# Three blocks of exponents, longer rings for h and u, and ScalarE's long stages in parts, in a selective-scan layer on one core

## What is computed

```
x = layernorm(x + scan(x));  x = layernorm(x + ffn(x))       # x: 2 x 1024 x 512

scan: xn = rmsnorm(x) * norm_w;  xn *= sigmoid((xn @ sel.T + b) * gate)
      delta, B, C = split(xn @ x_proj.T)                     # 128 each
      dt = softplus(delta @ dt_proj.T + dt_b);  A = -exp(A_log)   # A: 512 x 128
      for each of 1024 tokens:                               # h: 2 x 512 x 128
          h = exp(dt * A) * h + (dt * x) * B
          y = sum over the 128 states of h * C
      out = (y + x * D) @ out_proj.T
ffn:  (silu(x @ w_gate.T) * (x @ w_up.T)) @ w_down.T         # hidden 2048
```

## Time and profile before

| | us |
|---|---|
| three runs | 2697.46, 2687.02, 2690.41; median 2690.41 |
| the profiled execution | 2687.74 |
| its span | 2685.9 |
| VectorE busy | 2584.4 (96%) |
| TensorE busy | 2316.6 (86%) |
| ScalarE busy | 1708.6 (64%) |
| GpSimd busy | 1028.3 (38%) |

### The profile page before, as it was taken

How to read it: one execution, slowest core, us unless ns; L and a number is a source line. 1 busy time by engine, 2 the same in 40 slices (tenths; PEclk the granted TensorE clock), 3 DMA queues, 4 the chain that set the end, 5 groups by cost and what they waited for, 6 DMA issues and landing times.

```text
span 2685.9 us, 48350 instructions
## 1 busy us (share of the span) xinstructions
PE 2316.6 (86%) x17036; PEld 1290.5 (48%) x17036; DVE 2584.4 (96%) x4160; ACT 1708.6 (64%) x2229; POOL 1028.3 (38%) x1031
## 2 busy tenths in 40 slices
PE   7866678998789987899779997799977998899998
PEld 4322224554345543555345553455534554465567
DVE  6999999999999999999999999999999999999892
ACT  5687766667566665667656666566666667654643
POOL 2343333443434434344333443344333443344320
PEclk8999999999999989999889998899989999999899
DMA  4566665777667876678757786577866777788694
GB/s 171 197 213 227 228 236 211 281 277 270 237 223 277 284 266 223 238 275 292 254 195 247 279 290 243 201 267 277 278 241 209 279 279 271 239 289 308 228 357 151
DMA packets 192060, 672.16 MB, mean 250 GB/s; under 512 B 20944, under 2 KB 26064, under 8 KB 191824
## 3 DMA queue, kind: packets, MB, share of 16 engines
q1 hardware_dynamic: 152432, 544.02, 57.5%
q10 hardware_dynamic: 39392, 125.06, 13.3%
HBM read 660.61 MB, written 8.39 MB: 249 GB/s over the span
## 4 chain that ended last, share of the span: by engine, by line
PE 39%; DVE 28%; ACT 15%; issue 12%; DMA 6%; POOL 0%; ACTq 0%; DVEq 0%; POOLq 0%
DVE h L709 14%; PE banks L1200 11%; DVE banks L686 10%; PE banks L1036 10%; PE banks L1176 7%; PE banks L1276 7%; ACT a L981 6%; DVE h L706 4%; DMA u_bc<-u_scratch 4%; ACT L720 2%; DMA U<-in_xT 1%; PE banks L1128 1%; PE banks L1124 1%; ACT u_bc L1000 1%; ACT v L862 1%
## 5 line engine op out<-in xcount | busy, mean ns | idle before, releaser
L981 ACT ACTIVATE a<-banks 128x2048 f32<-128x2048 f32 x512 | 960.7, 1876 | 604.3 <-PE banks L1200 563.1
L686 DVE TENSOR_TENSOR banks<-a,h 128x512 f32<-128x512 f32 x2048 | 1324.1, 688 | 4.1 <-ACT a L981 4.1
L709 DVE SCALAR_TENSOR_TENSOR h<-u_bc,BCt,banks 128x512 f32<-128x512 f32 x1482 | 1038.2, 732 | 5.4 <-PE banks L1276 5.4
L581 POOL TENSOR_TENSOR dexp<-spread,dt 128x512 f32<-128x512 f32 x512 | 539.1, 1053 | 821.2 <-DVE banks L686 779.2
L1200 PE MATMUL banks<-dexp,A 32*128 32x256 f32 x8192 | 623.6, 421 | 150.6 <-ACT a L981 149.0
L1276 PE MATMUL banks<-h,cz 128*32 128x512 f32 x4096 | 667.9, 623 | 94.4 <-DVE h L706 64.7
L1200 PEld LDWEIGHTS banks<-dexp,A 32*128 32x128 f32 x8192 | 390.3, 195 | 484.4 <-ACT a L981 347.7
L1036 PE MATMUL banks<-vT,w_ring 128*128 128x256 f32 x1792 | 449.9, 394 | 7.6 <-ACT up L948 6.9
L1036 PEld LDWEIGHTS banks<-vT,w_ring 128*128 128x128 f32 x1792 | 323.8, 190 | 175.4 <-issue 118.2
L706 DVE TENSOR_TENSOR h<-u_bc,banks 128x512 f32<-128x512 f32 x566 | 367.5, 673 | 19.9 <-PE banks L1276 19.9
L593 POOL TENSOR_SCALAR u_bc<-u_bc,BCt 128x512 f32<-128x512 f32 x266 | 184.1, 692 | 404.6 <-DVE banks L686 394.3
(11 more groups left out here) (177 smaller groups left out, 1284.9 us busy)
## 6 DMA issues: line engine op xcount, KB each, us to landing
u_bc<-u_scratch SPq DMA_DIRECT2D x1021, 512.0 KB, 4.6
w_ring<-in_gu_w ACTq DMA_DIRECT2D x112, 512.0 KB, 5.5
w_ring<-in_down_w ACTq DMA_DIRECT2D x56, 512.0 KB, 5.7
a<-in_gu_w ACTq DMA_DIRECT2D x16, 512.0 KB, 12.7
a<-in_down_w ACTq DMA_DIRECT2D x8, 512.0 KB, 4.4
x_tok<-in_x_rows SPq DMA_DIRECT2D x15, 256.0 KB, 5.7
out_rows<-v ACTq DMA_DIRECT2D x15, 256.0 KB, 3.4
U<-in_xT ACTq DMA_DIRECT2D x7, 512.0 KB, 6.0
```

What stands on the lines that cost most here:

```text
L581: e.tensor_tensor(dexp[:, q % E_RING, :, :, :], spread[:, :].unsqueeze(1).unsqueeze(1).to_broadcast(shape), by_step[:, :, first:first + BS ...
L686: e.tensor_tensor(m_ps[:, b, :], a[:, blk % A_RING, b, s, :], h[:, (t - 1) % H_RING, b * D:(b + 1) * D], ALU.mult).then_inc(s_m, 1)
L709: e.scalar_tensor_tensor(h[:, t % H_RING, part], u_bc[:, t % U_RING, part], BCt[c % 2][:, 0, b * TB + tl:b * TB + tl + 1], m_ps[:, b, :], ...
L981: e.activation(dst.rearrange("p b t (x j) -> p x (b t) j", j=GP), src.rearrange("p g (i r j) -> p (g i) r j", i=PAIR, j=GP), ACT.Exp, scal ...
```

## The change

- `A_RING` 4 to 3, `H_RING` 6 to 8, `U_RING` 5 to 7. `DEXP_AHEAD` 8 to 6. With three blocks a tile has slot 4q-16: 8 and 6 steps before use.
- ScalarE scales u four steps ahead instead of two (`Z_AHEAD`), and in all chunks but the last, wherever the costs say that there is room; `quiet` goes.
- `sq`, `soft` and both layer norms are stages in parts (`sq` 0 and 1; `soft` in three thirds; `ln1`, `ln1b`, `ln2`, `ln2b`), with costs to match in `LOAD`. `layer_norm` becomes `center` and `normalize`, with two sets of statistics and two semaphores.
- Outside the last chunk GpSimd's gate pieces `gm` stand at least two slots later and `c1` one (`LAG`). Threads of equal slot are ordered by when they last had to wait.
- In the tail 12 tiles instead of 16 have their place in `a`: four issued at step 1017, four at 1021, four behind the loop, the other 12 as places come free.

```diff
-A_RING = 4
+A_RING = 3
-H_RING = 6
-U_RING = 5
+H_RING = 8
+U_RING = 7
+Z_AHEAD = 4
...
-TILES_IN_A = 16
+TILES_IN_A = 12
...
-USED_UP = {SEQ - 7: (0, 1), SEQ - 3: (2,)}
+USED_UP = {SEQ - 7: (0,), SEQ - 3: (1,)}
-DEXP_AHEAD = 8
+DEXP_AHEAD = 6
...
-    return max(2 * (q - DEXP_AHEAD), 5 + (4 * (q - DEXP_AHEAD) + 2) // 3)
+    return max(2 * (q - DEXP_AHEAD), 2 + (4 * (q - DEXP_AHEAD) + 2) // 3)
...
+LAG = {"gm": 2, "c1": 1}
...
-    yield from [("x_in", 0, 6), ("sq", 0, 4), ("ms", 0, 4), ("root", 0, 4)]
+    yield from [("x_in", 0, 6), ("sq", 0, 2), ("sq", 1, 2), ("ms", 0, 4), ("root", 0, 4)]
...
-        yield from [("dtp", j, 3), ("pre", j, 1), ("soft", j, 7), ("c1", j, 0), ("c2", j, 0), ("c3", j, 0), ("c4", j, 0)]
+        yield from [("dtp", j, 3), ("pre", j, 2), ("soft", 3 * j, 2), ("soft", 3 * j + 1, 3), ("soft", 3 * j + 2, 2), ("c1", j, 0), ("c2", j, 0), ("c3", j, 0), ("c4", j, 0)]
...
-        yield from [("outp", 2 * w, 3), ("outp", 2 * w + 1, 3 + wide), ("ln1", w, 2 * w if both else 4)]
+        yield from [("outp", 2 * w, 3), ("outp", 2 * w + 1, 3 + wide), ("ln1", w, 2 if both else 1), ("ln1b", w, 2 * w if both else 1)]
...
-        yield from [("back", w, 3 + wide), ("ln2", w, 1 + wide)]
+        yield from [("back", w, 3 + wide if x < LAST else 2), ("ln2", w, 1 + wide if x < LAST else 0), ("ln2b", w, 0)]
...
-        thread = min(threads, key=lambda t: t[0])
+        thread = min(threads, key=lambda t: (t[0], t[3]))
...
-            group = -(-slot // GROUP)
+            group = -(-(slot + (LAG.get(stage, 0) if c < LAST else 0)) // GROUP)
...
-        def quiet(t):
-
-            return t < TB or t < LAST * TB and 88 <= t % TB < 112
-
-        even = range(FIRST_Z, SEQ - 4, 2)
+        even = range(FIRST_Z, SEQ - Z_AHEAD, 2)
...
         on_act = {place: i for i, place in enumerate(
-            place for t in even if quiet(t) and light(t) and light(t - 2) for place in ((t + 2, 1), (t + 3, 0), (t + 3, 1)))}
+            place for t in even if t < LAST * TB and light(t) and light(t - 2)
+            for place in ((t + Z_AHEAD, 1), (t + Z_AHEAD + 1, 0), (t + Z_AHEAD + 1, 1)))}
...
+            def center(src, turn, x, w, n):
...
+            def normalize(x, w, n):
+                rows, st = v(x, w), stat[:, n % 2, :]
                 log_table()
...
-                        for place in ((t + 2, 0), (t + 2, 1)):
+                        for place in ((t + Z_AHEAD, 0), (t + Z_AHEAD, 1)):
```

More of the change, by code:

```diff
@@ L105, in stages_behind @@
     both, ws, wide = x < LAST, halves(x), int(x < LAST - 1)
-    ahead = W_RING if both else (TILES_14 if x == LAST else HB)
+    ahead = W_RING if both else (TILES_14 if x == LAST else TILES_IN_A)
     if x <= LAST:
@@ L160, in timetable @@
             thread[0] = emptied
+            thread[3] = emptied
             continue
@@ L296, in tile_of @@
                 flat = a[:, :, :, :, :].rearrange("p i b t d -> p (i b t d)")
-                return flat[:, j % TILES_IN_A * WT:(j % TILES_IN_A + 1) * WT]
+                block, part = divmod(j % TILES_IN_A, TILES_IN_A // A_RING)
+                place = (BLOCKS - A_RING + block) % A_RING * (TILES_IN_A // A_RING) + part
+                return flat[:, place * WT:(place + 1) * WT]
             return w_ring[:, (TILES * x + j) % W_RING, :]
@@ L728, in before @@
                                 ).then_inc(d_x, 16)
-                elif stage == "sq":
+                elif stage == "sq" and j == 0:
                     e.wait_ge(d_x, 16 * (x + 2))
@@ L782, in before @@
[L782 to L789 removed]
+                    half_d, part = j // 3, j % 3
@@ new lines, in before @@
+                    both = slice(2 * half_d, 2 * half_d + 2)
+                    n = 5 * (2 * (x - 1) + half_d)
+                    if part == 0:
+                        e.wait_ge(s_work, emptied("dtp", x, half_d))
+                        e.wait_ge(s_c2, 2 * x + half_d)
+                        if half_d == 0:
+                            e.wait_ge(d_us, 16 * BATCH * x)
+                        e.activation(t_exp, pre[:, :, :], ACT.Abs).then_inc(s_soft, 1)
+                        e.wait_ge(s_soft, n + 1)
+                        e.activation(pre[:, :, :], pre[:, :, :], ACT.Relu).then_inc(s_relu, 1)
+                    elif part == 1:
+                        log_table()
+                        e.activation(t_exp, t_exp, ACT.Exp, scale=-1.0).then_inc(s_soft, 1)
+                        e.wait_ge(s_soft, n + 2)
+                        if half_d == 0:
+                            e.wait_ge(s_xs, 2 * (x + 1))
+                        e.activation(T[:, both, :], t_exp, ACT.Ln, bias=one[:, :]).then_inc(s_soft, 1)
+                    else:
+                        e.wait_ge(s_soft, n + 3)
+                        e.activation(t_one, t_exp, ACT.Identity, bias=one[:, :]).then_inc(s_soft, 1)
+                        e.wait_ge(s_soft, n + 4)
+                        e.activation(t_one, t_one, ACT.Identity, bias=minus_one[:, :]).then_inc(s_soft, 1)
@@ L1028, in scalar @@
                         root_behind(stage, x, j)
-                    elif stage not in ("ymc", "vtc"):
+                    elif stage not in ("ymc", "vtc", "ln1b", "ln2b"):
                         behind(x, stage, j)
```

77 lines of the change are left out of this document (32 added, 45 removed).

## The result

The kernel after takes **2730.26 us** (median of 4 runs, 2725.65 to 2731.72), the kernel before 2688.72 (2682.63 to 2697.46): a ratio of 1.0145, 95% interval 1.0125 to 1.0164. The forecast of 2662 us had the wrong sign. The profiled execution has a span of 2727.3 us where before had 2685.9.

The account below looks back on a forecast made before the run. VectorE's own cadence plus waits was taken to bound the loop (VectorE 96% busy). 2687.7 - 6.0 - 26.9 - 3.0 + 10 = 2661.8, forecast 2662 us, bounds 2652 to 2672; the wider range ran from 2648 to 2682.

Parts of the forecast that it names:

- More halves scaled: VectorE's updates: ScalarE scales 117 more halves, 7.0 us gained less 1.0 for GpSimd collisions, net -6.0 us.
- The y ring: Eight places for h remove VectorE's waits for TensorE's y product, 25.3 us plus 1.6 for restarts: -26.9 us.
- Chunk 0 and the last chunk: GpSimd collisions with VectorE's products go: -1.0 us in chunk 0, -2.0 us in the last chunk.
- Edits at nothing: u places, later GpSimd pieces, split stages and u loads cost nothing; tail and last normalisation 0 to 4 us.
- item 5: New VectorE waits on ScalarE: exponent tiles 2.5 us (last chunk), scalings 13 us (chunks 1 to 6); +10 net, bounds 0 and 16.
- The tail: Stretch behind the loop, 65.4 us before: tiles issued by ScalarE and unit 7's queued tiles add 0 to 4 us.
- the 69 that I had named: Sign of being wrong: a tail over 69 us, where 65 to 66 was expected.
- B: Rival: three exponent blocks too short, late second tiles in slots 30 to 75 of chunks 1 to 7; 2700 to 2710, chance 0.09.
- A: Rival: ScalarE's carried lateness replaces TensorE's, the 25.3 us of waits only change name; about 2679 us, chance 0.18.
- C: Rival: scaled halves gain nothing, added ones falling beside GpSimd pieces; 2668 us, counted within the forecast's 0.65.
- the prediction's step at 1242.92: VectorE step with one scaled half taking 2.57 us instead of 2.46, its products beside a GpSimd piece: 0.11 lost.
- the rule, taken strictly: Shared SBUF port of VectorE and GpSimd: an unscaled update pair beside a piece would lose 0.12 us too.

Follow-up runs that it names:

- e6: Kernel after with the rule for scaled halves of the kernel before (521 updates without scaling instead of 683): 2719.76 us.
- e12: Kernel before with the new rings, scaling distance, 12 tail tiles and scaled-halves rule (800), plus products of exponents issued three slots ahead instead of two: 2652.2 us.
- e2: Kernel before with the change's rings, scaling four steps ahead and 12 tail tiles, keeping the old timetable and scaled-halves list: 2669.17 us.
- e10: Kernel before with one edit, TensorE issuing products of exponents three slots ahead of their exponentials instead of two: 2676.6 us.
- e5: Kernel after with one edit, TensorE issuing products of exponents three slots ahead of their exponentials instead of two: 2667.36 us.
- e3_one_slot: Kernel after with gate and up stages of units 0 to 5 one slot later, which also changes the scaled halves to 647: 2668.25 us.
- e8_slot_and_tail: e3_one_slot with the first four tail tiles issued behind step 1019 instead of 1017: 2664.44 us.

## Why the prediction was wrong, point by point

1. **More halves scaled: right in size, wrong as a gain.** 683 updates, nominal 7.0 us less. But each added scaling is also a thing that a late ScalarE delivers late: at this timetable e6 shows a net loss of 10.5 us, while with the exponents first e12 keeps the 14.0 us that its 234 further halves are worth (waits of 7.6 us, for 9.3 in e2).

2. **The y ring: right.** 25.3 us of waits became 0.8, and e2_rings, the rings alone, gains 20.2. I took TensorE's lateness behind these waits as given. e10 shows that half of it was the order of its queue, for which no ring was needed.

3. **Chunk 0 and the last chunk: half right.** Chunk 0 went from 318.6 to 313.7. The last chunk, forecast near 325, took 335.0. Its y waits fell from 9.0 us to 0.8, but waits on exponent tiles (2.0 and 1.1 us) and on GpSimd's scaling at step 996 (3.3) came in their place, 7.2 us in all, and the rest rose by 1.9. e2 has 336.8, e5 334.5: it is neither the timetable nor the order alone, and no kernel of the study has less than 331.8. What holds the last chunk back stays open.

4. **"Edits at nothing": this is the step that failed.** I wrote that the pieces two slots later wait less for ScalarE. By the rules of the timetable the entry for `gm` moves no piece in any chunk. What moved were the gates in front of them, from odd slots to even ones, by edits of stages that I had costed one by one as splitting without adding. The first gate pieces (L524), which by my words would wait less for ScalarE, waited 101.7 us for it; before, those of these chunks waited for VectorE alone. I looked at what each moved stage waits for and at ScalarE's room, and not at **which instruction of another stream stands right behind it in TensorE's queue**. The 39.4 us of rest are this step, and so are the waits of item 5: with the exponents first (e5) the rest is back at 10.7 and the waits are 7.5. The tail, bound 4 us, cost 4.6, and at 70.0 it is over the 69 that I had named as a sign of being wrong: four queued tiles were read rightly, the six slots of unit 7 not at all.

5. **What is late next: right place, wrong cause, too small.** Waits on scalings near step 34 did come (7.5 us for 13 foreseen), in the last chunk those on exponent tiles (3.1 for 2.5). The largest, 12.9 us near step 124, I had not seen, nor the waits of 0.70 us on an exponent tile at step 123 of chunks 1, 2, 4, 5 and 6:

```profile
1650.94 1.30 DVE L688 TENSOR_TENSOR banks<-a,h 128x512 f32<-128x512 f32 x2 [0.70 <-ACT a L998]
```

   None of those on scalings comes from ScalarE's whole stretches, as I had it: e5 takes them all away without touching ScalarE's order.

Of the rivals, B had the sign, but its ring of three blocks has little part in it: outside the last chunk the waits on exponent tiles are the 3.5 us of step 123, they are in neither e5 nor e2, which have three blocks too, and e2 gains. A named carried lateness and gave it no more than the waits of before. Only C had VectorE's own instructions take longer, at 0.11 us a step; here it was 0.77.

## What to carry to other kernels

When a timetable by hand moves a stage, list for every in-order queue which neighbour it now stands ahead of and behind, and ask whether the first of the two waits for something that is behind the other on the next engine; a product that feeds the bound engine goes ahead of one that can wait for a bank. A ring or a scaling ahead that seems to help against lateness may only hide an order that makes it: here one slot in one table was worth 12 us before, 29 with all scalings, and 63 after. Test such a shift by the least edit, alone, before sizes are tuned around it.

## What the runs showed of the hardware

**A late GpSimd costs VectorE only under its products, and only where it began first.** The products read `a` and `h`, both in SBUF; the updates read one operand from a bank. The pieces and diagonal tiles of e5 above, 1.28 and 1.04 us, start with an update pair, and its steps there stay at 2.52; the diagonal tile of 1.05 us under a product pair of the kernel after made 2.06 of 1.29, and the piece under the end of the pair before took 1.76 instead of 1.28. The Trainium skill (SBUF — State Buffer, "Who interferes with whom") has this split: an instruction of VectorE with two SBUF inputs contends with GpSimd's reads, one with a single SBUF input doesn't. The trace agrees.

Which of the two pays goes by which began first. VectorE, then GpSimd, at steps 95 and 96 of chunk 4 of the kernel after:

```profile
1577.10 1.29 DVE L688 TENSOR_TENSOR banks<-a,h 128x512 f32<-128x512 f32 x2
...
1579.62 2.06 DVE L688 TENSOR_TENSOR banks<-a,h 128x512 f32<-128x512 f32 x2
```

```profile
1577.09 2.20 POOL L583 TENSOR_TENSOR dexp<-spread,dt 128x512 f32<-128x512 f32 x1
1579.25 1.27 POOL L527 TENSOR_TENSOR gated<-gated,up 128x512 f32<-128x512 f32 x1
```

The diagonal tile that starts together with the products takes 2.20 us instead of 1.05 and leaves them at 1.29; the piece that starts 0.37 us ahead of them keeps its 1.27 and makes 2.06 of 1.29. In chunks 1 to 6 GpSimd began 0.13 to 0.46 us ahead in all 41 long steps, and the products stayed at 1.3 us in the 29 steps where it began at most 0.07 ahead of them, or behind their start, and still ran under them. VectorE lost the overlap less some 0.13 us: 0.77 of 0.91 in step 65, 0.11 of 0.23 at the prediction's step at 1242.92, and nothing of the 0.11 left over beside unscaled pairs. That offset is why the rule, taken strictly, gave the prediction 0.12 where the trace has none.

**TensorE's granted clock fell behind one gap of the cross-wait, and not behind another.** An earlier gate of the kernel after, in order of time, and the stretches before and in it (granted clock in the column behind the five engines):

```profile
1477.26 3.60 PE L1053 MATMUL banks<-vT,w_ring 128*128 128x256 f32 x8 [1.83 <-ACT up L963]
```

```profile
1476.00:1477.26 1.26, 0.01 (x1) 0.01 (x1) 1.26 (x3) 1.26 (x5) 0.77 (x1) 1.00 0.82 270
1477.26:1480.79 3.53, 3.53 (x9) 2.32 (x9) 3.53 (x7) 0.33 (x1) 1.30 (x2) 0.53 0.80 288
```

TensorE had idled 1.83 us; the next eight matmuls ran at 0.53 of full speed, near the lower of its two levels, 1.2 of 2.4 GHz, and took 3.60 us, not 1.99. At 1494.70, behind the same gap, they took 1.99. So a gap can cost 1.6 us more than itself. Chunk 4 has a clock of 0.94; the mean of the execution is 0.955 after and 0.979 in e5_exp_first, with the same matmuls. The kernel before, which has next to none of these gaps, has 0.956, so a lower clock doesn't explain that the kernel after is slower than it. How much of the 63 us between after and e5 is clock and how much the waits themselves was not separated.

**Mean durations of VectorE's groups differ between executions of equal cadence.** Its products average 705 ns in e3_one_slot and 688 in e8_slot_and_tail, 35 us over 2048 of them, while the loops differ by 3.1 us and most steps are 2.40, 2.46 and 2.52 in both. The cadence is to be read from starts, not from means.
